# Layer 1 attention: both LayerNorm scalings on GpSimd, row transposes into another PSUM bank, router weights behind the head scaling, residual rows loaded first

## The reference, cut to what matters

```python
def _layernorm(x, axis=-1, eps=1e-05):
    m = jnp.mean(x, axis=axis, keepdims=True)
    v = jnp.var(x, axis=axis, keepdims=True)
    return (x - m) / jnp.sqrt(v + eps)
...
x = x + jnp.tanh(g_xattn[1]) * _L1_xattn_ref(_layernorm(x, axis=-1), ctx_1024, mask_BxS2_bk0, L1_xattn_W_Q, ...)
x = x + jnp.tanh(g_ffn[1]) * _L1_ffn_ref(_layernorm(x, axis=-1), L1_ffn_gate_w, L1_ffn_w_gate_up, ...)
# _L1_xattn_ref: 16 heads, softmax over 77 keys
A = jax.nn.softmax(E / jnp.sqrt(jnp.float32(KEY_SIZE)), axis=-1)
Y = Yp.transpose(0, 2, 1, 3).reshape(b, sq, h * dv) @ W_O
# _L1_ffn_ref: 32 experts, 4 of them for a row
logits = x @ gate_w.T
probs = jax.nn.softmax(logits, axis=-1)
topk_w, topk_idx = jax.lax.top_k(probs, K)
topk_w = topk_w / jnp.sum(topk_w, axis=-1, keepdims=True)
```

## Time and profile before

| | |
|---|---|
| time, median of 3 runs | 1118.74 us (1117.76 to 1120.73) |
| the profiled execution: its own time / its span | 1107.31 us / 1105.2 us |
| the stage of the change, from its first DMA to the last row sent | 542.5 to 907 us |
| PE busy over the span | 905.5 us (82%) |
| DVE busy | 660.3 us (60%) |
| ACT busy | 465.6 us (42%) |
| POOL busy | 553.4 us (50%) |

### The profile page before, as it was taken

One profiled execution on the slowest core, in us unless ns is written; L12 is line 12 of the kernel. 1 busy time (PEld: TensorE's weight loads), 2 busy tenths in 40 slices (PEclk: granted clock), 3 DMA queues, 4 the chain that ended last, 5 costly groups with the idle time before them and its releaser, 6 DMA issues. The chain is left out here.

```text
span 1105.2 us, 18625 instructions
## 1 busy us (share of the span) xinstructions
PE 905.5 (82%) x5465; PEld 763.1 (69%) x5465; DVE 660.3 (60%) x2223; ACT 465.6 (42%) x1721; POOL 553.4 (50%) x592
## 2 busy tenths in 40 slices
PE   4997858999999688898169999999999977999900
PEld 3673547788788487788158888888888845787800
DVE  3604036776767455566258899999999933444421
ACT  1414642322322245455147677777777711222200
POOL 1300123555555435555526766666666541677762
PEclk8969978888989799999679999999999989999955
DMA  9522884578776977767498934413340004999789
GB/s 307 189 81 86 239 239 121 170 211 204 238 211 177 233 223 235 239 217 223 166 228 209 229 87 165 162 68 129 113 132 14 14 11 126 229 227 250 122 188 159
DMA packets 163957, 189.71 MB, mean 172 GB/s; under 512 B 16035, under 2 KB 145209, under 8 KB 163858
## 3 DMA queue, kind: packets, MB, share of 16 engines
q1 hardware_dynamic: 112882, 121.87, 37.9%
q0 software_dynamic: 33792, 46.46, 19.4%
q10 hardware_dynamic: 17184, 20.19, 5.4%
HBM read 96.19 MB, written 103.63 MB: 181 GB/s over the span
## 5 line engine op out<-in xcount | busy, mean ns | idle before, releaser
L1717 ACT ACTIVATE att<-bank,mx 128x77 f32<-128x77 f32 x512 | 159.8, 343 | 17.1 <-DVE mx L1780 15.0
L1680 POOL DMA_INDIRECT slots_d<-rows,place x128 | 127.9, 1000 | 71.8 <-DVE place L1868 40.6
L1717 ACT ACTIVATION_READ_ACCUMULATOR att<-bank,mx 128x1 f32 x512 | 114.9, 224 | 0.0
L960 POOL DMA_INDIRECT y_d<-rows,targets x78 | 79.3, 1017 | 67.7 <-DVE rows L1291 41.4
L1932 PE MATMUL bank<-vwo_hi,attT_hi 128*128 128x256 f32 x320 | 93.9, 293 | 3.9 <-DVE attT_lo L1795 2.0
L1933 PE MATMUL bank<-vwo_lo,attT_hi 128*128 128x256 f32 x320 | 91.2, 285 | 0.0
L1934 PE MATMUL bank<-vwo_hi,attT_lo 128*128 128x256 f32 x320 | 91.0, 284 | 0.0
L1932 PE MATMUL bank<-wqk_hi,xa_hi 128*128 128x462 f32 (+1 forms) x192 | 76.4, 398 | 6.3 <-DVE xa_lo L1785 4.5
L1704 ACT ACTIVATE attT_hi<-bank 128x512 fp32r<-128x512 f32 x64 | 39.0, 610 | 78.7 <-PE bank L1973 78.7
L1313 PE MATMUL bank<-wd_hi,act_hi 128*128 128x256 f32 (+1 forms) x206 | 70.0, 340 | 2.2 <-issue 1.3
L927 POOL DMA_INDIRECT slots_d<-rows,place x64 | 63.7, 996 | 15.9 <-issue 15.7
(11 more groups left out here) (302 smaller groups left out, 2724.5 us busy)
## 6 DMA issues: line engine op xcount, KB each, us to landing
expert_gate_up<-in_wgu SPq DMA_DIRECT2D x40, 256.0 KB
rows<-slots_d SPq DMA_DIRECT2D x39, 260.0 KB
slots_d<-zrow SPq DMA_DIRECT2D x8, 1168.0 KB
expert_rows<-slots_d SPq DMA_DIRECT2D x32, 292.0 KB
x_res<-y_d POOLq DMA_DIRECT2D x14, 512.0 KB, 12.0
expert_down<-in_wd SPq DMA_DIRECT2D x40, 128.0 KB
wqk_d<-wqk SPq DMA_DIRECT2D x32, 154.0 KB, 3.6
vwo_d<-vwo SPq DMA_DIRECT2D x16, 308.0 KB
```

Of the source, the lines that this page charges most:

```text
L960: pool.indirect_dma_start(y0_d, bass.IndirectOffsetOnAxis(ap=tgt0[:, s % NY0, b:b + 1], axis=0), y_rows(s, b), None, bounds_check=T * K0 - ...
L1680: pool.indirect_dma_start(slots_d, bass.IndirectOffsetOnAxis(ap=place[:, n % 3, k:k + 1], axis=0), rows[:, n % 3, :], None, bounds_check=S ...
L1717: last = act.activation(att[:, par, h * S:(h + 1) * S], bank[:, a, i * S:(i + 1) * S], ACT.Exp, scale=-1.0, bias=mx[:, par, h:h + 1], accu ...
```

## The change

Five things are moved; no arithmetic is added or dropped.

1. `norm_a` and `norm_b`, the two instructions per tile that apply mean and deviation, go from VectorE to GpSimd, each right behind its `rstd`. GpSimd's list in a step is then: adding DMAs, `rstd` and `norm_a` of tile n+1, `rstd` and `norm_b` of tile n-2, four indirect DMAs of tile n-3. VectorE keeps the copy of the row number (`row_number`), and `stats("b")` waits for an older `norm_b`.
2. The transposes of `rows` are written into the second half of bank 5 in place of bank 6. `transpose_a` no longer waits for `b_xT`, and the transposes of `rows` wait for `av_added` instead of `a_xT`.
3. The router weights (`wn`, L1901) and their reciprocal come behind the scaling of the first 12 heads.
4. At the start of the block SyncE loads the rows of tiles 2 and 3 and the first `vwo` ahead of the small weights, and TensorE waits for these only before the first logits.
5. At the start VectorE makes the low part of tile 0 (`low_a(0, 0)`) before it waits for the rows of tile 1.

```diff
@@ sync
                     load_scores(0)
                     first_rows(1)
+                    first_rows(2)
+                    first_rows(3)
+                    load_values(0)
                     sp.dma_start(wr1[:], io["wr1"].rearrange("(k p) n -> p k n", p=P)).then_inc(w3_in, 16)
                     sp.dma_start(sgu[:], io["sgu1"].rearrange("(k p) n -> p k n", p=P)).then_inc(w3_in, 16)
                     sp.dma_start(sdn[:], io["sd1"]).then_inc(w3_in, 16)
-                    first_rows(2)
-                    load_values(0)
-                    first_rows(3)
@@ gpsimd
+                    def norm_a(n, par):
+                        pool.wait_ge(ln["a"]["ready"], n + 1)
+                        want(pool, a_T, n - 1)
+                        pool.tensor_scalar(xa[:, par, 0:D - 1], x[:, n, 0:D - 1], ln["a"]["mv"][:, par, 0:1],
+                                           ln["a"]["rstd"][:, par, :], ALU.subtract, ALU.mult).then_inc(a_xn, 1)
+
+                    def norm_b(n, par):
+                        want(pool, sent[n % 3], 16 * K1 * (n // 3))
+                        want(pool, b_T, n - 2)
+                        pool.wait_ge(ln["b"]["ready"], n + 1)
+                        pool.tensor_scalar(rows[:, n % 3, 0:D], tile(n), ln["b"]["mv"][:, par, 0:1], ln["b"]["rstd"][:, par, :],
+                                           ALU.subtract, ALU.mult).then_inc(b_xn, 1)
...
                         if scores and n + 1 < TILES:
                             rstd("a", n + 1, 1 - par)
+                            norm_a(n + 1, 1 - par)
                         if routes:
                             rstd("b", n - 2, par)
+                            norm_b(n - 2, par)
@@ scalar
-                            act.activation(xbT[:, :, (n - 2) * P:(n - 1) * P], bank[:, 6, 0:D].rearrange("p (k t) -> p k t", k=KD),
+                            act.activation(xbT[:, :, (n - 2) * P:(n - 1) * P], bank[:, 5, D:2 * D].rearrange("p (k t) -> p k t", k=KD),
@@ vector, first()
-                        dve.wait_ge(c3, 1)
-                        norm_a(0, 0)
+                        low_a(0, 0)
                         experts_added(1)
...
                         dve.wait_ge(c3, 8)
-                        low_a(0, 0)
@@ vector, step()
                         if added:
+                            want(dve, b_xn, n - 3)
                             stats("b", n - 2, par)
...
-                        if ahead:
-                            norm_a(n + 1, 1 - par)
...
                         if routes:
-                            norm_b(r, par)
+                            row_number(r)
...
@@ tensor
                         pe.wait_ge(a_xn, n + 1)
-                        want(pe, b_xT, n - 2)
                         want(pe, a_xT, n)
...
                         transpose_a(0, 0)
-                        pe.wait_ge(w3_in, 48)
                         pe.wait_ge(c3, 8)
...
                             pe.wait_ge(b_xn, r + 1)
-                            pe.wait_ge(a_xT, min(n + 1, TILES))
+                            pe.wait_ge(av_added, r + 1)
                             for k in range(KD):
-                                last = pe.transpose(bank[:, 6, k * P:(k + 1) * P], rows[:, r % 3, k * P:(k + 1) * P], ident[:])
+                                last = pe.transpose(bank[:, 5, D + k * P:D + (k + 1) * P], rows[:, r % 3, k * P:(k + 1) * P], ident[:])
...
                         if routes:
+                            if r == 0:
+                                pe.wait_ge(w3_in, 48)
                             pe.wait_ge(b_xT, r + 1)
```

24 lines of the change are left out of this document (7 added, 17 removed).

## The result

The changed kernel is slower: 1134.47 us (median of 4, 1131.98 to 1138.63) against 1118.25 of the kernel before (median of 4, 1117.13 to 1120.73) on the same chip, ratio 1.0153 with a 95% interval of 1.0115 to 1.0191. The forecast was 1107.6 with a range up to 1122; the result lies outside it, on the other side of no change.

What follows compares the result with a forecast made beforehand. A VectorE-ScalarE-VectorE loop sets the 10.06 us step, TensorE close behind; -10.6 (middle) - 3.0 (start) + 1.5 (early) + 1.0 (end) = -11.1 us, to 1107.6 us, range 1100 to 1122.

Steps and rivals of the forecast that it cites:

- What bounds the kernel now: Middle steps: a loop VectorE, ScalarE, VectorE of 6.38 and 3.68 us sets the 10.06 us step, TensorE close behind.
- the 0.32 us that the loop was to lose with `norm_a`: Middle steps, second leg of the loop: norm_a leaves VectorE, which shortens the leg by 0.32 us.
- TensorE's floor of 9.44 to 9.74: Middle steps: TensorE's work plus 0 to 0.3 us of remaining wait, above the loop's 9.3; step taken as 9.6.
- The first leg: Middle steps, VectorE's first minimum to its head scaling: 6.38 us falls to about 5.9; moved router weights cost nothing new.
- Does GpSimd keep up?: Middle steps: GpSimd's lap without waits is 9.0 us, with scalings at 0.93 each, and fits under 9.6.
- -10.6: Middle steps' gain: 23 steps at 0.46 us less each, with ends of -7 and -14 us.
- no wait by half a microsecond: Middle steps: norm_b on GpSimd ends near 797.8, TensorE wants it at 798.37, so it is in time.
- Rival 2: GpSimd scalings cost 1.65 us, lap 10.4, total 1135; TensorE waits at rows' transposes, GpSimd never idles; chance 0.07.
- Rival 1: Middle steps: norm_a on GpSimd shuts out VectorE's second head scaling, +5.5 us, 1123 or 1124 in all; chance 0.11.
- The early steps: Steps 3 to 7, adding DMAs: GpSimd laps of 11.8 and 10.4 us, +1.5 us in all, ends 0 and +8.3.
- The start: Start of the block: tile 3's rows land early, removing waits of VectorE and TensorE; -3.0 us, ends 0 and -5.
- The end: Steps 32 and 33: TensorE waits for norm_b, GpSimd needs 0.93 for VectorE's 0.41; +1.0 us for both.

Runs made afterwards that it cites:

- 11: Kernel before with the bank change and norm_a on GpSimd; norm_b on VectorE, router weights and start as before: ratio 0.9911 to the kernel before.
- 8: Changed kernel with norm_b back on VectorE and the router weights again ahead of the first head scaling: ratio 0.9894 to the kernel before.
- the seventh: Kernel before with the bank change alone (transposes of rows into bank 5, waits changed): ratio 0.9907 to the kernel before.
- 2: Changed kernel with only norm_b back on VectorE, norm_a staying on GpSimd: 1112.48 us, ratio 0.9937 to the kernel before.
- 10: Kernel before with the start (loading order, early low part of tile 0) and the bank change; both norms on VectorE: ratio 0.9881 to the kernel before.
- 1: Changed kernel with both norm_a and norm_b back on VectorE at their old places: ratio 0.998 to the kernel before.
- the sixth kernel: Kernel before with the start alone (loading order, early low part of tile 0): ratio 0.9989 to the kernel before.
- the twelfth kernel: Changed kernel with VectorE's two head scalings cut to one head each, 14 of 16 heads unscaled: ratio 0.9892 to the kernel before.
- the fifth: Changed kernel with router weights and their reciprocal again ahead of the first head scaling, both norms on GpSimd: ratio 1.0106 to the kernel before.

## Why the prediction was wrong, step by step

**What bounds the kernel now: nearly right.** The prediction read a loop VectorE, ScalarE, VectorE. The bank alone, which touches no VectorE instruction, takes the step from 10.06 to 9.70; so the wait of TensorE before `transpose_a`, through which ScalarE's `xa_hi` waited, was a link of the loop, as the prediction used it. Of the 0.32 us that the loop was to lose with `norm_a`, only 0.08 came, since TensorE's floor lies there.

**TensorE's floor of 9.44 to 9.74, taken as 9.6: right.** Kernels 11 and 8, in which TensorE waits for nothing in the middle steps or nearly so, have 9.61 and 9.62. The rest of TensorE's wait, 0 to 0.3 at the logits, is 5.2 us over 20 times in the seventh.

**The first leg, shortened by the scaling no longer standing behind `ew`: wrong in sign.** I priced the third part on ScalarE's side (it lets the scaling start earlier) and at nothing on VectorE's. With VectorE full it costs 0.15 (8 against 2) to at most 0.2 us (10 against 1). That alone would not have cost the forecast its sign: 9.77 is still under 10.06.

**"Does GpSimd keep up?": the step that failed.** Its lap was the right quantity; two of its terms were too small.

1. *The scaling.* Between 0.93 and 1.65 I took 0.93 to 1.1, "as the nearest row", though I had written that L404 has half the operands and half the arithmetic. It is 1.27 and 1.24, in the middle: +0.65 for two.
2. *The meetings.* The prediction saw `veps_a` take 0.99 us in place of 0.21 until VectorE's scaling had ended, called that "no work", and put `veps_a` into the lap with 0.21. No work it is; but the time passes for GpSimd. In a lap with 1.3 us of waiting elsewhere it costs nothing, and in one without it costs all. The 0.78 us that I struck out are nearly the 0.89 (0.48 on the fourth DMA, 0.41 on `veps_a`) that came back.

With both, by the prediction's own sum: 9.0 + 0.65 + 0.78 = 10.43, above 10.06, and slower by 22 x 0.37 = +8.1 in the middle in place of -10.6. TensorE's wait at the transposes of `rows`, which the prediction had as no wait by half a microsecond, follows from this: with GpSimd's lap as the period, `norm_b` comes as late as the lap makes it. Rival 2 had the mechanism and the sign that would show it. That its time (1135) is the measured one is luck: it has a scaling of 1.65 us and no meetings, and measured are 1.25 and 0.9 us of meetings. And its threshold, 1.46 us a scaling, was worked out from the lap of 9.0 and so was too high: with the 0.78 in the lap it is 0.93 + (10.06 - 9.78) / 2 = 1.07. Its chance of 0.07 was a chance for "dear", when "not cheap" was enough.

**Rival 1: its loss isn't there.** It named exclusion, but with another pair and the other direction. Its pair, `norm_a` and the second head scaling, doesn't meet in the changed kernel: `norm_a` starts at 801.49, and the scaling has ended at 800.65. In the second kernel the pair does meet, and VectorE is first by 0.09 us, the harmless side of the race; `norm_a` takes 1.55 us (801.81, shown above), and VectorE as ever:

```profile
801.72 0.48 DVE L1816 TENSOR_TENSOR att<-att,den 128x308 f32<-128x308 f32 x1
```

What meets in the changed kernel are the fourth DMA and `veps_a` with the two head scalings, and there GpSimd stands, since its DMAs come late and the scaling is there first.

**The early steps: right in mechanism, too small by the same two terms.** Laps of GpSimd by its first DMAs at 598.05, 611.33, 624.90 and 636.59 are 13.28, 13.57 and 11.69 us, where the prediction had 11.8, 11.8 and 10.4. The difference of 1.3 to 1.8 is 0.65 for the scalings and a fourth DMA of 1.35 to 1.89 us (0.97 in the kernel before):

```profile
602.10 1.70 POOL L1696 DMA_INDIRECT slots_d<-rows,place  x1 [0.30 <-issue]
```

Of the +5.7, about 2 come with the start and the bank (kernels 1 and 10), the rest with the norms.

**The start: right in size** (-3.1 for -3.0), and 4.2 alone. VectorE no longer waits for the rows of tile 3, as said. But TensorE's pauses moved more than they went: in place of 1.89 and 2.02 us before its values it now stands 6.70 us for `norm_a` of GpSimd (at 578.66), and in the sixth kernel 4.92 for `attT_lo`. The prediction had neither, so the fit of the sum is in part luck. That the gain could be given back later wasn't in the prediction either.

**The end: right in its own term** (1.3 us more of waiting in step 32 and none in step 33, for +1.0), but +2.4 came from the clock, which the prediction had looked at only at the start.

## What to carry to other kernels

When work is moved to an engine that looks half idle, write down its whole lap with the durations that its instructions have *there*, its stalls beside other engines included: such a stall is free only as long as the engine waits for someone anyway, and it moves to another instruction when the phase shifts. Of a price between two bounds, ask first from which price the result turns, with all the other terms at their bad ends; if that point lies between the bounds, the forecast has no sign yet. And try the parts of a change one by one: here one of five (the bank, four lines) carried nearly the whole gain, one (the weights' place) cost 0.15 to 0.2 us a step, and one (both norms on GpSimd) cost more than all the others gave.

## What the runs showed of the hardware

- GpSimd's scaling of 128 x 255 float32 values takes 0.96 us with one scalar operand and one arithmetic step, 1.27 with two; 1.54 where a VectorE scaling runs beside it (second experiment).
- An indirect DMA of 128 rows on GpSimd, the fourth of a step, takes 0.97 us. One that starts inside VectorE's head scaling (a multiplication of 128 x 924, 1.12 us) ends 0.84 or 0.85 us after that one's end. One that starts ahead of it isn't delayed, and doesn't delay it. An adding DMA, which isn't indirect, isn't delayed either way (1.47 us beside the scaling and without it).
- The other way round, VectorE's `rows` instruction of 32 columns takes 0.51 us in place of 0.30 and ends at 800.11, with the DMA's 800.10, in the changed kernel. In the twelfth kernel the same instruction, 0.08 us behind the start of the fourth DMA, takes 0.30, and so it does in the fifth, where it starts at 783.81, just as the scaling ends and the DMA beside it gets on. In the changed kernel it starts 0.35 us behind the scaling's end. How far the DMA has got may be what tells them apart; no run here varies that alone.
- TensorE's granted clock in the same step of the program was between 0.69 and 1.00 from kernel to kernel, worth up to 2.6 us (10.89 against 8.27), with waits ahead of it of 1.76 and 1.89.
